# A modulated linear and a mixture of experts on one core: the start, the first expert tiles, the weight reloads and the last scatters rearranged

## The reference

```python
x = x + (x * ys) @ weight * d                # modulated linear, ys and d from the condition
shared = silu(xf @ w1) * (xf @ w3) @ w2      # 4096 tokens, D 512, hidden 1024
s = sigmoid(concat(xf, tf) @ router_W)
topk_idx = top_k(s + router_bias, 2)         # 8 experts, 2 per token, gates normed
h = gelu(einsum('nc,ech->enh', xf, W1e))     # expert hidden 512
y = einsum('enh,ehc->enc', h, W2e)
out = x + (shared + sum of gate * y) / 3
```

## Time and profile before

| | |
|---|---|
| median of 3 runs | 1032.83 us (1032.2 to 1033.69) |
| profiled execution, its own time | 1032.92 us |
| its span | 1031.1 us |
| granted TensorE clock, mean | 0.998 |
| PE busy | 1016.8 us, 99% |
| DVE, ACT, POOL busy | 50%, 28%, 31% |
| chain that ended last, share of PE | 97% |
| moved by DMA | 228.67 MB, mean 222 GB/s |

### The profile page before, as it was taken

One profiled execution on the slowest core, in us unless ns is written; L12 is line 12 of the kernel. 1 busy time (PEld: TensorE's weight loads), 2 busy tenths in 40 slices (PEclk: granted clock), 3 DMA queues, 4 the chain that ended last, 5 costly groups with the idle time before them and its releaser, 6 DMA issues.

```text
span 1031.1 us, 14537 instructions
## 1 busy us (share of the span) xinstructions
PE 1016.8 (99%) x4696; PEld 837.9 (81%) x4696; DVE 517.0 (50%) x836; ACT 292.6 (28%) x461; POOL 314.7 (31%) x389
## 2 busy tenths in 40 slices
PE   9999999999999999999999999999999999999996
PEld 7888788888888888888888887888888888888884
DVE  6555546567334443334322215565665566566653
ACT  3223432222222222223221113333333332333231
POOL 0000000001122342332323401454554655555533
PEclk9999999999999999999999999999999999999999
DMA  5766565636878888899974676999988999999985
GB/s 176 246 227 229 197 204 184 225 111 182 288 232 300 263 296 298 287 269 300 338 213 143 205 199 211 208 224 236 208 154 187 219 216 224 221 229 228 227 195 74
DMA packets 133262, 228.67 MB, mean 222 GB/s; under 512 B 29040, under 2 KB 83952, under 8 KB 125104
## 3 DMA queue, kind: packets, MB, share of 16 engines
q1 hardware_dynamic: 60256, 144.05, 43.7%
q0 software_dynamic: 31328, 64.11, 27.5%
q10 hardware_dynamic: 41616, 19.69, 8.3%
HBM read 112.85 MB, written 98.38 MB: 205 GB/s over the span
## 4 chain that ended last, share of the span: by engine, by line
PE 97%; DMA 1%; issue 1%; DVE 0%; POOLq 0%; ACTq 0%; POOL 0%; ACT 0%; DVEq 0%
PE banks L557 12%; PE banks L558 12%; PE banks L559 12%; PE banks L488 11%; PE banks L490 11%; PE banks L489 11%; PE banks L502 6%; PE banks L504 6%; PE banks L503 6%; PE banks L425 3%; PE banks L426 2%; PE banks L427 2%; DMA out<-ys,slot 1%; PE banks L465 1%; PE banks L471 1%
## 5 line engine op out<-in xcount | busy, mean ns | idle before, releaser
L488 PE MATMUL banks<-xh,w 128*128 128x512 f32 x512 | 199.6, 390 | 0.6 <-DVE xl L761 0.6
L490 PE MATMUL banks<-xh,w 128*128 128x512 f32 x512 | 199.2, 389 | 0.0
L489 PE MATMUL banks<-xl,w 128*128 128x512 f32 x512 | 199.2, 389 | 0.0
L1231 POOL DMA_INDIRECT out<-ys,slot x71 | 116.3, 1637 | 187.6 <-DVE ys L1130 106.1
L834 DVE SCALAR_TENSOR_TENSOR gm<-sil,banks 128x512 f32<-128x512 f32 x64 | 44.0, 687 | 250.4 <-ACT sil L642 241.5
L642 ACT ACTIVATE sil<-banks 128x512 f32<-128x512 f32 x64 | 38.3, 598 | 336.6 <-PE banks L490 325.2
L1217 POOL DMA_DIRECT2D xg<-xs_d x136 | 100.6, 1138 | 49.4 <-DVE xgt L1091 49.4
L488 PEld LDWEIGHTS banks<-xh,w 128*128 128x128 f32 x512 | 96.1, 188 | 20.9 <-issue 1.1
L490 PEld LDWEIGHTS banks<-xh,w 128*128 128x128 f32 x512 | 96.1, 188 | 20.0
L557 PE MATMUL banks<-we,xgth 128*128 x284 | 110.7, 390 | 1.7 <-issue 1.6
L489 PEld LDWEIGHTS banks<-xl,w 128*128 128x128 f32 x512 | 96.1, 188 | 19.8
(11 more groups left out here) (177 smaller groups left out, 1449.1 us busy)
## 6 DMA issues: line engine op xcount, KB each, us to landing
we_d<-ehl SPq DMA_DIRECT2D x32, 1024.0 KB
we<-we_d SPq DMA_DIRECT2D x48, 512.0 KB
hturn<-hid ACTq DMA_DIRECT2D x284, 64.0 KB
xg<-xs_d POOLq DMA_DIRECT2D x136, 128.0 KB
eraw<-expert_w SPq DMA_DIRECT2D x32, 512.0 KB
x1t_d<-x1t SPq DMA_DIRECT2D x8, 1024.0 KB, 8.8
xin<-x1t_d SPq DMA_DIRECT2D x8, 1024.0 KB, 8.6
x_d<-x1tok SPq DMA_DIRECT2D x32, 256.0 KB
```

What stands on the lines that cost most here:

```text
L488: pe.matmul(ps[hc % 2][:, :], w_hi, xh[:, j, c, :], start=(c == 0), stop=False)
L489: pe.matmul(ps[hc % 2][:, :], w_hi, xl[:, j, c, :], start=False, stop=False)
L490: last = pe.matmul(ps[hc % 2][:, :], w_lo, xh[:, j, c, :], start=False, stop=(c == DC - 1))
L1231: pool.indirect_dma_start(out[:, :], IO(slot[:, t, 0:1], 0), ys[:, t % RING, :], None, compute_op=ALU.add).then_inc(added[t % 2], 16)
```

## The change

1. **Start.** Ten matmuls on zeros, not 20. Input chunks 1 to 3 are issued on SyncE's queue between the weight chunks. ScalarE's first square root, which brings its table, works on zeros and not on the condition's squares.
2. **`move_h(1)`** is issued by SyncE, behind the last store of the shared stage and ahead of the weight parts, not by ScalarE.
3. **Scatter semaphores.** `added` has four, one for each buffer of `ys`. Scatter t waits for t-4, and for t-1, t-2 and t-3 only where their expert is another. The table has three rows, made at VectorE's turn 4, not one row made at turn 1; GpSimd reads three values per scatter.
4. **Weight release.** For turns 4 to 7 the first half waits for the last `matmul1` of the place (`mm1_done`), the second for its last `matmul2`, and each half is one transfer of 2 MB.

```diff
+                if c:
+                    sp.dma_start(xin[:, 0, c, :], xT[0, :, c, :]).then_inc(x0_in[c], 16)
...
+            move_h(sp, BY_SYNC)
             for i in range(4, HRING):
                 load_in_parts(i, first[i // 2], slice(i // 2, i // 2 + 1))
             for r in range(WRING, E):
                 e, place, over = table(0, r, E - 1), table(1, r, WRING - 1), table(2, r, TILES)
-                sp.wait_ge(mm2_done, over + 1)
-                for i in (2 * r, 2 * r + 1):
-                    load_in_parts(i % HRING, e, bass.ds(place, 1))
+                for i, used in ((2 * r, mm1_done), (2 * r + 1, mm2_done)):
+                    sp.wait_ge(used, over + 1)
+                    load_weight(i, e, bass.ds(place, 1))
+                    sp.wait_ge(we_in[i % HRING], parts_before[i % HRING] + 16)
+                    sp.sem_inc(weights_in, 1)
...
-            for _ in range(20):
+            for _ in range(10):
                 pe.matmul(lin_ps[4][:, :], zeros[:, 0:P], zeros[:, :], start=True, stop=True)
...
-            for c in range(DC):
-                act.dma_start(xin[:, 0, c, :], xT[0, :, c, :]).then_inc(x0_in[c], 16)
-            act.wait_ge(prep, 2)
-            act.activation(dtmp[:, :, :], modsq, ACT.Sqrt).then_inc(root, 1)
+            act.dma_start(xin[:, 0, 0, :], xT[0, :, 0, :]).then_inc(x0_in[0], 16)
+            act.wait_ge(zeros_done, 1)
+            act.activation(dtmp[:, 0, :], zeros[:, 0:BATCH].bitcast(FP32), ACT.Sqrt).then_inc(root, 1)
...
-                if t < TILES:
-                    move_h(t)
+                if t < TILES and t != BY_SYNC:
+                    move_h(act, t)
...
             def scatter_waits():
 
-                then(dve.tensor_scalar(wait_for[0:1, :], cst[0:1, C_TIX:C_TIX + TILES], 1.0, None, ALU.add))
-                then(dve.tensor_scalar(wait_for[0:1, :], wait_for[0:1, :], 1, 255, ALU.logical_shift_right, ALU.bitwise_and))
-                then(dve.tensor_tensor(same[0:1, 1:TILES], turn_of[0:1, 1:TILES], turn_of[0:1, 0:TILES - 1], ALU.is_equal))
-                then(dve.tensor_tensor(same[0:1, 1:TILES], wait_for[0:1, 1:TILES], same[0:1, 1:TILES], ALU.subtract))
-                dve.tensor_scalar(wait_for[0:1, 1:TILES], same[0:1, 1:TILES], 16.0, None, ALU.mult).then_inc(waits_done, 1)
+                for b in range(1, RING):
+                    turns_, count = same[0:1, b - 1, b:TILES], wait_for[0:1, b - 1, b:TILES]
+                    then(dve.tensor_scalar(count, cst[0:1, C_TIX:C_TIX + TILES - b], float(RING), None, ALU.add))
+                    then(dve.tensor_scalar(count, count, 2, 255, ALU.logical_shift_right, ALU.bitwise_and))
+                    then(dve.tensor_tensor(turns_, turn_of[0:1, b:TILES], turn_of[0:1, 0:TILES - b], ALU.is_equal))
+                    then(dve.tensor_tensor(turns_, count, turns_, ALU.subtract))
+                    dve.tensor_scalar(count, turns_, 16.0, None, ALU.mult).then_inc(waits_done, 1)
...
                 if t == 1:
                     dve.wait_ge(slots_in, 16 * SUB)
+                if t == RING:
                     scatter_waits()
...
-                if t > 1:
-                    pool.wait_ge(added[t % 2], 16 * (t // 2))
-                if 0 < t < 3:
-                    pool.wait_ge(added[(t - 1) % 2], 16)
-                elif t:
-                    landed = pool.value_load(wait_for[0:1, t:t + 1], min_val=16, max_val=16 * (TILES // 2 + 2))
-                    pool.wait_ge(added[(t - 1) % 2], landed)
-                    pool.sem_inc(scatter_free, 1)
+                if t >= RING:
+                    pool.wait_ge(added[t % RING], 16 * (t // RING))
+                landed = {b: pool.value_load(wait_for[0:1, b - 1, t:t + 1], min_val=16, max_val=16 * (TILES // RING + 2))
+                          for b in range(1, RING) if t - b >= RING}
+                for b in range(1, min(t, RING - 1) + 1):
+                    if t - b < RING:
+                        pool.wait_ge(added[(t - b) % RING], 16)
+                    else:
+                        pool.wait_ge(added[(t - b) % RING], landed[b])
+                        pool.sem_inc(scatter_free, 1)
```

More of the change, by code:

```diff
@@ L35 @@
 LAG = TURN_LAG + 1
+BY_SYNC = 1
 Q = 32
@@ L114, in shared_moe_kernel @@
         xgt = sb("xgt", [2, DC, P], FP32, 192)
-        wait_for = sb("wait_for", [TILES], INT32, 196)
-        same = sb("same", [TILES], INT32, 196.5)
+        wait_for = sb("wait_for", [RING - 1, TILES], INT32, 196)
+        same = sb("same", [RING - 1, TILES], INT32, 197)
         x1tok = sb("x1tok", [BLK // Q, DC, Q], FP32, 168)
@@ L231, in shared_moe_kernel, with move_h @@
         waits_done, scatter_free = sem("waits_done"), sem("scatter_free")
-        added = [sem(f"added{j}") for j in range(2)]
+        added = [sem(f"added{j}") for j in range(RING)]
         block = ctx.enter_context(nc.Block())
+        def move_h(engine, t):
+            engine.wait_ge(hid_done, t + 1 + 2)
+            for g in range(P // Q):
+                engine.dma_start(hturn[g * Q:(g + 1) * Q, t % RING], hid[:, t % RING, g * P:(g + 1) * P]).then_inc(h_moved[t % RING], 16)
         @block.sync
@@ L383, in _ @@
                 e, place, over = table(0, r, E - 1), table(1, r, WRING - 1), table(2, r, TILES)
-                sp.wait_ge(mm2_done, over + 1)
-                for i in (2 * r, 2 * r + 1):
-                    load_in_parts(i % HRING, e, bass.ds(place, 1))
+                for i, used in ((2 * r, mm1_done), (2 * r + 1, mm2_done)):
[3 more added lines that the diff above has]
+                    sp.sem_inc(weights_in, 1)
             sp.wait_ge(out_stored, 16 * NBLK)
-            for j in range(2):
-                sp.wait_ge(added[j], 16 * ((TILES - j + 1) // 2))
+            for j in range(RING):
+                sp.wait_ge(added[j], 16 * ((TILES - j + RING - 1) // RING))
         @block.tensor
@@ L394, in _ @@
             pe.sem_inc(lin_done, 1)
+            pe.sem_inc(mm1_done, 1)
             pe.sem_inc(mm2_done, 1)
@@ L615, in _ @@
                 act.wait_ge(x0_in[c], 16)
+                if c == 0:
+                    act.wait_ge(prep, 1)
                 x_high(0, c, mod[:, c, 0:1])
@@ L699, in hidden @@
             def hidden(t):
-                act.wait_ge(mm1_done, t + 1)
+                act.wait_ge(mm1_done, t + 1 + 1)
                 if t >= RING:
@@ L705, in hidden @@
                                h_ps[t % 2][:, :].rearrange("p (c g n) -> p c g n", g=SUB, n=Q), ACT.Gelu).then_inc(hid_done, 1)
[L707 to L711, removed]
             def h_high_of(t):
@@ L1220, in scatter @@
             def scatter(t):
[L1222 to L1229 removed]
+                if t >= RING:
[8 more added lines that the diff above has]
+                        pool.sem_inc(scatter_free, 1)
                 pool.wait_ge(ys_done, t + 1 + 2)
                 pool.indirect_dma_start(out[:, :], IO(slot[:, t, 0:1], 0), ys[:, t % RING, :], None,
[L1232 removed]
+                                        compute_op=ALU.add).then_inc(added[t % RING], 16)
             for m in (2, 3, 4):
                 load_pair(m)
[L1236 removed]
             pool.wait_ge(pads_in, 16)
@@ L1241, in _ @@
                     load_pair(t // 2 + 4)
+                if t == RING + 1:
+                    pool.wait_ge(waits_done, RING - 1)
                 scatter(t)
```

4 lines of the change are left out of this document (1 added, 3 removed).

## The result

| | before | with the change |
|---|---|---|
| median of 5 runs each | 1033.22 us (1032.2 to 1035.85) | 1048.9 us (1045.12 to 1050.35) |
| ratio, 95% interval | | 1.0138 (1.0116 to 1.0159) |
| profiled execution, its span | 1032.92, 1031.1 us | 1045.12, 1043.3 us |
| granted TensorE clock, mean | 0.998 | 0.992 |

The change makes the kernel slower by 1.4%. The forecast was 1029.0. The profiled execution is the fastest of the five, so its 12.2 us more are less than the median's 15.7.

What follows compares the result with a forecast made beforehand. TensorE was taken as the bound, never waiting for weights; 1032.92 less 0.8 (start), plus 0.1 (first tiles), less 3.35 (scatters), weight release 0, gave 1028.9, stated as 1029.0 us; range 1026.8 to 1031.6.

Steps and rivals of the forecast that it cites:

- Weight release: Reloads of turns 4 to 7: first half may start some 22 us earlier, nobody needs it; taken as 0.
- The 2 MB transfers hold up the tiles: Rival, 9%: from 757 us whole transfers make `hturn` or `xg` late; eight at 1 us each, 1037 us.
- the cover: TensorE's margin, read at tile 65's `hidtl`: 3.4 us of lateness on VectorE cost nothing.
- Start: Before the first shared chunks: 0.8 us gained, bounds 1.4 gained and 0.9 lost; 0.6 by the skill's rule.
- the squares: Gate at `demodulation` in the start: squares ended at 15.93 us, expected 0.5 to 1 us earlier.
- The second block's input: In the start, behind three more issues on SyncE: taken 0.6 us later, near 15.7.
- First tiles: Pause at 641.7 us: 1.55 us could be won, but the moved table delays tile 5; net 0.1 us lost.
- The slow read: `look_up(4)` at 641.7 us, 1571 ns once: 70% not to recur; rival that it recurs, 17%, 1030.1 us.
- Scatters: End of the kernel: last scatters follow `ys` sooner; 3.35 us gained, bounds 2.5 and 3.7.

Runs made afterwards that it cites:

- part 4 alone: Kernel before with only the fourth point, halves released one by one, each one 2 MB transfer: 1052.57 us, ratio 1.0199.
- two of 1 MB: The change with each weight half in two waited transfers of 1 MB, rows of 8 KB, new release kept: 1030.87 us, ratio 0.9981.
- parts: The change with each weight half in four waited transfers of 512 KB, new release kept: 1031.3 us, ratio 0.998.
- long rows: The change with each half in four waited 512 KB transfers over 64 partitions, rows of 8 KB, new release kept: 1032.45 us, ratio 0.999.
- start alone: Kernel before with only the first point, the new start: 1032.28 us, ratio 0.9989.
- part 3 alone: Kernel before with only the third point, four scatter semaphores and the three-row table at turn 4: 1033.58 us, ratio 1.0003.
- parts together: The change with each half as four 512 KB transfers issued together and waited for once: 1037.68 us with the new release, 1037.54 with the old.
- whole transfers with the old release: The change with single 2 MB transfers kept, but both halves released by the last second product as before: 1040.77 us, ratio 1.0067.

## Why the prediction was wrong

**The step that failed** is "Weight release", with "Nobody needs it. Cost nothing" and "I take 0". It costs 17.6 us by the medians. The mechanism is the one of the rival *The 2 MB transfers hold up the tiles*, which I gave 9%; the runs show it: part 4 alone makes the kernel before slower by 18.9 us, and with a wait inside each half nothing of it is left (two of 1 MB: 1030.87; parts: 1031.3; long rows: 1032.45, which is not told apart from the parts).

**The argument against that rival** was that no row shows TensorE waiting though the DMA share is 1.02. The row was read wrongly. It says that the DMA engines were occupied, not how long a small transfer waits for its turn: in the same 860 to 880 us the share is 1.08 with the change and 1.09 with two transfers of 1 MB, and the one kernel stops and the other does not. That TensorE waited for nothing says that lateness was under the cover, not how near to it. What I should have read stood in the waits of GpSimd and VectorE before: GpSimd already waited 58.2 us for landings in this stretch, once 7.3, and VectorE already waited 1.4 us for `xg`. VectorE's own margin was therefore zero in places, and the cover of 3.4 us was all there was. The traces show where it ends. A wait of VectorE for `hturn` comes out at TensorE as a pause 3.1 to 3.2 us shorter (8.62 gave 5.45, 7.15 gave 3.99, 6.00 gave 2.89, 5.13 gave 2.00, 4.51 gave 1.35), a wait for `xg` as one 4.1 to 4.7 us shorter (12.95 gave 8.46, 10.06 gave 5.37, 6.33 gave 1.73), and no wait under 2.9 us gave one by itself. Up to that edge lateness is free, past it each microsecond counts, and more with the clock. I took the price of a transfer as a slope from zero, and it was a cliff.

**The size.** The rival had 1 us for each of eight transfers, 8 us in all. In the profiled execution about 14.4 us came in few places: two long pauses of 5.5 and 4.15 us. I had also not seen the way by GpSimd's queue, where a scatter that waits for the landing of another expert's holds back the loads of inputs behind it. Issuing those earlier gives 7.3 us back. And I had left out the lower clock here; behind the two long pauses it costs 3.4 us.

**Start.** Forecast 0.8, measured 1.23 in the profile of the change and 1.0 by the medians alone. The chunks came sooner, as the step had it: the squares end at 12.03 + 2.49 = 14.52, 1.4 us earlier than before. The second block's input was forecast 0.6 us later, "near 15.7"; it came at 14.16, earlier than before. The new order issues the transfers in the sequence in which they are needed, and the load behind them lost nothing. By the Trainium skill ("DMA: Bandwidth & Descriptors", Issuing engines are not separate DMA queues) the issuer changes no bandwidth; that this would leave the start at 0.6 us is not borne out. What changed is the order as well as the issuer, and I put the gain down to the order; no run separates the two.

**First tiles.** The table took 644.46 to 647.69, 3.2 us (forecast 3.4), and `xgtl` ended at 648.88; TensorE paused 1.0 us ahead of tile 5 (forecast 1.65). The slow read did not recur: the same look-up took 0.91 us against 1.571 and TensorE paused 0.55 us there, and in the other kernels with `move_h(1)` on SyncE it is about the same, while with `move_h(1)` on ScalarE it took 1.42 us (start alone), 1.69 us (part 3 alone) and 1.80 us (part 4 alone). So part 2 did its work: between 640 and 646 us TensorE's lead over the kernel before grew from 1.2 to 2.2 us. Net 0.4 us lost against 0.1. That the table was what ate this gain is shown: made earlier, 1.5 us come back, and the pause is gone.

**Scatters.** Forecast 3.35, measured 1.7 us in the profile. The wait for t-2 is gone, as forecast. But that the two table reads more "fit under the 1.55 us in which the engine still works on the one before" is wrong: scatters now follow each other by 1037.63 - 1034.86 = 2.77 us, where 1.85 was taken, and the last stands 1.86 us behind its `ys`. The reads and the waits that need them run in the queue one after another once the engine is there. With the reads made beforehand the last scatter goes 0.28 us behind `ys`, and the end comes 1.3 us sooner in the trace. Parts 1 to 3 in all bring 2.0 us, not 4.0.

**What stays open.** With whole transfers the earlier release adds 8.1 us (1040.77 to 1048.9); with parts, waited for or not, it adds nothing (1031.45 and 1031.3; 1037.54 and 1037.68). One difference stands in the traces: with the early release a 2 MB transfer is issued at 780.72, just ahead of scatter 24 (781.57), for whose landing scatter 25 waits, and with the old one at 783.2, once the place is free; from scatter 24 to 25 it is 12.8 and 11.9 us (8.1 before). The 0.9 us between those two is far less than the 8.1 to be explained, so this is a hint and no more. Also open is why long rows make a full queue so much worse (1037.68 to 1048.9). The Trainium skill ("DMA: Bandwidth & Descriptors", Queues, rings and completion order) says that an engine turns from queue to queue by packets of several descriptors; then the wait of a small transfer grows with the length of the others' rows. The order of the medians fits that (waited, together, whole), and in 785 to 875 us a piece of 8 KB took a DMA engine 0.32 us in the median where one of 4 KB (parts together) took 0.17; but no run shows an engine's turns. And it is open whether the gaps or the lower pace that comes with them save the tiles.

## What to carry to other kernels

A background load of the same bytes can be free or dear by the way it is issued: put waits into it and test the pace, since here 1 MB waited for was free and 2 MB cost 17.6 us for some 30 us less of loading that nobody needed. Nothing was measured between 1 and 2 MB, and the edge will lie elsewhere in a kernel with another cover. The Trainium skill ("DMA: Bandwidth & Descriptors", Rules for kernel authors) asks for 1 MiB and more per transfer for bandwidth; the bandwidth came here (78 GB/s in parts, about 110 at 1 MB, 140 at 2 MB), and at 2 MB the kernel got slower. Ahead of such a change, read how late the small transfers on other queues already are and what margin is behind them, above all where an engine's queue has a wait for a landing ahead of a prefetch: a bound engine that never waits says nothing about the distance to the edge.

## What the runs showed of the hardware

- TensorE's granted clock fell to the lower level behind pauses of 8.5, 5.5, 5.4, 4.1, 4.0, 2.9, 2.2 and 2.0 us, and behind one of 1.87 us (two of 1 MB, at 687 us). It did not fall behind pauses of 1.86 us (whole transfers with the old release, at the same place), 1.73, 1.70 and 1.55 us, all as the waits view counts them. So the length of the pause alone does not decide near 1.9 us. At the lower level a matmul of 512 columns takes 0.43 us, at the higher 0.23.
- On TensorE's load queue the read of a tile's expert took 0.30 us in the median and up to 1.57 us in the kernel before, the read of its weight place 0.63 us in the median in the same kernel. The longest came at one look-up, and only in kernels in which ScalarE issues `move_h(1)` (1.57, 1.42, 1.69 and 1.80 us; 0.7 to 0.9 us in seven kernels in which SyncE issues it).
- On GpSimd the last scatters follow each other by 2.77 us with three reads and their waits between them, by 2.07 with one (before, 1016.74 to 1018.81) and by 1.85 with the reads made ahead.
- The new order of scatters has a cost of its own near the first tiles. The rule that a scatter waits only for t-4 and for other experts does not hold for the first of them: the code has scatters 1 to 6 wait for whichever of the scatters 0 to 3 are among the three before them, of the same expert or not. So scatter 3 now waits for the landing of scatter 2; it goes at 674.0 us in the kernel with parts and the new release, and went at 668.3 before. GpSimd then comes late to the next inputs, and TensorE paused 0.4 to 1.9 us near 685 us in five of the kernels (the two with parts, the whole transfers with the old release, the long rows, the two of 1 MB) but not in the change itself. All of these run the same code up to there, so this pause comes and goes from one execution to the next.
